# How far a gathering GpSimd may run ahead in the last two of three passes

## The chip, the cores and the metric

The kernel runs on one core of a Trainium2 chip. The time is that of the device for one execution, in microseconds (us), and stands as a median of several runs. Engines are named PE (TensorE, matmul; PEld is its weight load), DVE (VectorE), ACT (ScalarE), POOL (GpSimd) and SP (SyncE, which only issues DMAs here).

## The reference

A graph has 6250 nodes with 128 features and 100000 edges sorted by destination. Two layers of graph convolution are followed by one attention layer; both blocks end in a residual and a layer norm.

```
norm = dinv[src] * ew * dinv[dst]                    # dinv = 1/sqrt(deg), self-loops added
h  = relu(segment_sum((x@W1)[src] * norm, dst) + b1)
h  = sigmoid(segment_sum((h@W2)[src] * norm, dst) + b2)
x2 = layernorm(x + h)
z  = x2 @ fc_w.T;  rh = edge_attr @ fc_r_w.T
e  = leaky(z[src]@a0 + z[dst]@a1 + rh@a2)            # one score for each edge
alpha = softmax of e over the edges of each dst
agg = segment_sum(alpha * (z[src] + rh), dst)
out = layernorm(x2 + relu(agg + z @ loop_w))
```

## The kernel before

The edges are cut into 782 tiles of 128, and the tiles into 98 groups of 8. Each of the three sums over edges is one pass over the groups. In a pass, GpSimd fetches the source rows of each tile with one indirect DMA (128 rows, a gather), from x1_d in pass 0, h1_d in pass 1 and x2_d in pass 2, into `ring`. The ring has 18 groups (R) in passes 0 and 1 and 12 (R2) in pass 2. VectorE builds a one-hot matrix S of the destinations, weighted (`build_S`, L1608), and PE multiplies gathered rows by it into a window of PSUM (`sum_group`, L858; in pass 2 also the edge attributes, L860). After the last matmul of a group PE raises the semaphore `summed`.

Not all tiles are gathered. Sets of 32 tiles are permuted by source and looked up in a copy of the table in SBUF: ACT makes one-hots (`slot_onehot`, from a broadcast load of low_d that SP issues), PE looks rows up (`look_up`, L898), ACT copies them, VectorE makes slots (`make_slots`, L1681) and PE sums them (`sum_slots`, L910). Pass 0 has six such sets and gathers 74 groups, pass 1 nine sets and 62 groups (590 and 494 gathers). In pass 2 three sets (12 groups: 38 to 41, 62 to 65, 86 to 89) are treated in a like way, and 86 groups are gathered (686 gathers).

Each engine has its program written out; semaphores are the only tie. GpSimd's program is `gathers` for pass 0, 1 and 2 (L704 to L728). Ahead of a group it waits until its place in the ring has been summed, ahead of each gather until the one six before it has landed. A pass's gathers begin when the last blocks of its table are stored.

During pass 1 and after it come the picks: each edge needs the score z[dst]@a1 of its destination. `begin_pick` (L1825) compares a broadcast load of destination bits (dlo_d, issued by SP, 512 KB for a pair of groups after pass 1) with the partition index, PE multiplies with a small table (`pick`, L944), and `end_pick` (L1834) sums the result and raises `picked`, once for two groups, 49 times in all. 36 pairs are done within pass 1; the other 13 follow it, with three dot products of edge attributes (`rh_dot`, L1709) and the tables of nodes (`node_table`, L1797 to L1812) between them. Then pass 2's softmax starts: chunks of 2, then 4 groups. `scores(c)` (L1917) reads the gathered rows of its chunk and of one tile of the next (17 tiles for chunk 0, up to the 49th for chunk 1), and `softmax` (L1955 to L1978) gives the weights for `build_S`.

Of the kernel before, what the change touches and what calls it, by code (L numbers as in the profile page):

```python
# [16 lines left out]
G = -(-T // GT)  # L17
# [11 lines left out]
R = 18  # L29
# [22 lines left out]
def tiles(q):  # L52
    return range(q * GT, min((q + 1) * GT, T))
# [147 lines left out]
assert sorted(ORDER) == list(range(len(CH))) and all(XS[r] + 29 <= CLOSES[SETK[XR[r]]] for r in range(len(XR)))  # L201
assert all(XS[r] + 28 <= XS[r + 1] and X_AT[r] + 1 < CHUNK[XC[r]] for r in range(len(XR) - 1))
LANES = 6
PARTS = {G - 2: (0, 4, GT), G - 1: (0, 3, 5, T - (G - 1) * GT)}


# [31 lines left out]
def build(nc, x, src, dst, edge_attr, edge_weight, W1, b1, W2, b2, fc_w, fc_r_w, attn_w, loop_w, out):  # L238
    ctx = ExitStack()
    with ctx:  # L240
# [3 lines left out]
        def sem(name):  # L244
            return ctx.enter_context(nc.semaphore(name))
# [173 lines left out]
        def s(name):  # L419
            if name not in sems:  # L420
                sems[name] = sem(name)
            return sems[name]

        landed = [sem(f"landed{j}") for j in range(LANES)]
        rh_loaded = [sem(f"rh_loaded{j}") for j in range(NR)]
# [8 lines left out]
        def turn(p, t):  # L434

            return sum(len(tiles(i)) for g in GL[:p] for i in g) + (GL[p] if p < 2 else GATHERED).index(t // GT) * GT + t % GT

        def ring_at(p, h):

            return (AT[p] + h) % R if p < 2 else GATHERED.index(h) % R2  # L440

        def await_rows(eng, p, ts):

            for i in [turn(p, t) for t in ts][-LANES:]:
                eng.wait_ge(landed[i % LANES], 16 * (i // LANES + 1))

# [9 lines left out]
        def stored(sems, k):  # L456

            return sems[k % 2], 16 * (k // 2 + 1)

        def any_wide(eng):  # L460
            eng.wait_ge(s("flag_made"), 1)
            return eng.If(eng.value_load(flag[0:1, 0:1], min_val=0, max_val=1) != 0)

        def ecols(g):
            return bass.ds(g * GT, GT)
# [228 lines left out]
        @block.gpsimd  # L694
        def _(pool):
            nc.gpsimd.memset(srcR[:, EB - 1, :], 0).then_inc(s("pads_set"), 1)
            nc.gpsimd.memset(dstR[:, EB - 1, :], int(FAR)).then_inc(s("pads_set"), 1)
            nc.gpsimd.memset(ewR[:, EB - 1, :], 0.0).then_inc(s("pads_set"), 1)
            nc.gpsimd.iota(iota_i, [[1, NARROW]], base=0, channel_multiplier=0).then_inc(s("iota_made"), 1)
            nc.gpsimd.iota(pidx_i[:, :], [[1, 1]], base=0, channel_multiplier=1).then_inc(s("iota_made"), 1)  # L700
            nc.gpsimd.memset(rows[:, NB - 1, 0:D], 0.0).then_inc(s("pads_set"), 1)
            nc.gpsimd.iota(baseI, [[GT, TC]], base=-MARGIN, channel_multiplier=0).then_inc(s("iota_made"), 1)

            def gathers(p, table, width):  # L704
                for h, q in enumerate(GL[p] if p < 2 else GATHERED):
                    gg = AT[p] + h
                    if p == 0 and h == R0:
                        pool.wait_ge(s("x1_stored"), 16 * 7)
                    if p == 0 and h == R - 9:
                        pool.wait_ge(s("setup_done"), 1)  # L710
                        pool.wait_ge(s("dpad_stored"), 64)
                    if p == 2 and h >= R2:
                        pool.wait_ge(s("summed"), AT[2] + GATHERED[h - R2] + 1)
                    elif p < 2 and gg >= R:
                        pool.wait_ge(s("summed"), gg - R + 1)
                    for k, t in enumerate(tiles(q)):
                        i = turn(p, t)
                        if i >= LANES:
                            pool.wait_ge(landed[i % LANES], 16 * (i // LANES))
                        pool.indirect_dma_start(ring[:, ring_at(p, h if p < 2 else q), k, 0:width], None, (x if p == 0 and h < R0 else table)[:, :],  # L720
                                                bass.IndirectOffsetOnAxis(ap=srcC[:, t:t + 1], axis=0)).then_inc(landed[i % LANES], 16)
                    if p == 0 and h == P // GT - 1:
                        pool.wait_ge(s("cols_copied"), 7)

            pool.wait_ge(s("cols_copied"), 1)
            gathers(0, x1_d, D)
            pool.wait_ge(*stored(h1_stored, NA - 2))
            pool.wait_ge(*stored(h1_stored, NA - 1))  # L728
            gathers(1, h1_d, D)
            pool.wait_ge(*stored(x2_stored, NA - 2))  # L730
            pool.wait_ge(*stored(x2_stored, NA - 1))
            gathers(2, x2_d, XW)

            def wide_gathers(n, phase, table, width, stored):
                pool.wait_ge(stored, 16)
                with pool.Fori(0, G) as g:
                    pool.wait_ge(s("wide_group"), g + (phase * G + 1))
                    pool.sem_inc(s("pool_passed"))
                    nc.gpsimd.tensor_copy(stageW, srcC[:, ecols(g)]).then_inc(s("wide_staged"), 1)
                    pool.wait_ge(s("wide_staged"), g + (n * G + 1))  # L740
                    pool.sem_inc(s("pool_passed"))
                    for k in range(GT):
                        pool.indirect_dma_start(wring[:, k, 0:width], None, table[:, :],
                                                bass.IndirectOffsetOnAxis(ap=stageW[:, k:k + 1], axis=0)).then_inc(s("wide_gathered"), 16)

            with any_wide(pool):
                pool.wait_ge(s("out_stored"), 16 * NA)
                nc.gpsimd.iota(baseWi, [[GT, TC]], base=-MARGIN, channel_multiplier=0).then_inc(s("wide_iota"), 1)
                wide_gathers(0, 1, x1_d, D, s("wide_x1_stored"))
                wide_gathers(1, 2, h1_d, D, s("wide_h1_stored"))  # L750
                wide_gathers(2, 3, x2_d, XW, s("wide_x2_stored"))
                wide_gathers(3, 4, x2_d, D, s("wide_x2_stored"))

        @block.tensor
        def _(pe):
# [86 lines left out]
            def sum_group(p, h):  # L842
                gg = AT[p] + h
                q = SEQ[gg][1]
                parts = PARTS[q] if p < 2 and q in PARTS else (0, len(tiles(q)))
                if p == 2:
# [1413 lines left out]
```

## Time and profile before

| | |
|---|---|
| Runs | 2405.14 us median of 3 (2404.65 to 2409.71) |
| The profiled execution | span 3348.6 us; no other time of it is given |
| Mean granted PE clock | 0.787 |
| Busy share | PE 61%, PEld 53%, DVE 55%, POOL 51%, ACT 28% |
| Instructions | 40819; 1781 of them on POOL |

The profiled execution is a single one, recorded by the hardware. Its span is 943.5 us longer than the median of the runs. In timelines a row is: start, length, engine, line, operation, out<-in, and in brackets the engine's idle time just before and what ended it. "issue" there is time in which the engine waited for nothing that the profile shows; "remote" or "unknown queue" is a wait whose releaser isn't known. Pass 0 ends, and pass 1's gathers begin, at 1179.7 us; pass 2's gathers begin at 2117.07.

### The profile page before, as it was taken

How to read it: one execution, taken by the hardware profiler on the slowest of the kernel's cores; microseconds unless marked ns; L12 is line 12 of the kernel's file. 1: busy time of each engine (PE TensorE's matmuls, PEld its weight loads, DVE VectorE, ACT ScalarE, POOL GpSimd, SP SyncE). 2: the span in 40 equal slices, each digit the busy share in tenths (PEclk: the TensorE clock that was granted, in tenths of full speed). 3: DMA queues.
4: the chain of work that ended last, by engine and by line, in shares of the span. 5: the costliest groups of instructions: out<-in, count | busy, mean ns of one | idle time of the engine just before them, and what ended most of it. 6: DMA issues, size and time to landing. Idle time of an engine off the chain costs nothing.

```text
span 3348.6 us, 40819 instructions
## 1 busy us (share of the span) xinstructions
PE 2044.2 (61%) x13384; PEld 1762.3 (53%) x13384; DVE 1834.8 (55%) x7005; ACT 946.7 (28%) x1754; POOL 1718.9 (51%) x1781
## 2 busy tenths in 40 slices
PE   1416444588888911177777888106677667756786
PEld 1315433566767811166666677005666666645675
DVE  3626435577779810156656687217654564546457
ACT  1316000122233300033333444101254225412541
POOL 7351666665550067466556500555766646663640
PEclk9857667798999955588988899557778778877888
DMA  4112221222221122123333332525343534443431
GB/s 118 30 42 66 69 61 47 61 61 63 60 62 32 51 76 53 41 74 86 99 103 102 93 91 80 138 62 147 97 103 97 134 93 102 108 117 79 103 97 34
DMA packets 272093, 270.54 MB, mean 81 GB/s; under 512 B 43454, under 2 KB 218709, under 8 KB 271862
## 3 DMA queue, kind: packets, MB, share of 16 engines
q1 hardware_dynamic: 201790, 143.87, 15.1%
q0 software_dynamic: 56640, 117.52, 14.8%
q10 hardware_dynamic: 13448, 6.47, 0.7%
q8 instruction: 112, 1.84, 0.2%
q14 instruction: 103, 0.84, 0.1%
HBM read 254.14 MB, written 13.97 MB: 80 GB/s over the span
## 4 chain that ended last, share of the span: by engine, by line
PE 35%; DVE 21%; another core or an unknown queue 21%; issue 15%; ACT 4%; SPq 1%; DMA 1%; POOL 1%; ACTq 0%; DVEq 0%; POOLq 0%
PE ps L858 9%; PE ps L910 8%; DVE SR L1608 5%; PE ps L860 3%; PE ps L898 3%; PE ps L1045 2%; DVE U L1709 2%; DVE SR L1681 2%; DVE SR L1571 1%; PE ps L885 1%; DVE U L1648 1%; PE ps L1029 1%; POOL ring L720 1%; PE ps L792 1%
## 5 line engine op out<-in xcount | busy, mean ns | idle before, releaser
L720 POOL DMA_INDIRECT ring<-x_d,srcC x1132 | 1109.7, 980 | 971.2 <-issue 579.0
L858 PE MATMUL ps<-SR,ring 128*128 128x128 f32 x3540 | 672.5, 320 | 205.0 <-issue 132.0
L858 PEld LDWEIGHTS ps<-SR,ring 128*128 128x128 f32 x3540 | 580.5, 231 | 238.9 <-issue 178.9
L720 POOL DMA_INDIRECT ring<-h_d,srcC x494 | 469.9, 951 | 457.1 <-DMA h_d<-Lb 170.9
L1681 DVE TENSOR_SCALAR SR<-iota_r,cols 128x288 f32<-128x288 f32 x735 | 365.0, 564 | 303.9 <-remote 226.6
L910 PE MATMUL ps<-SR 128*128 128x288 f32 x1470 | 416.6, 435 | 118.1 <-ACT SR L1232 75.3
L910 PEld LDWEIGHTS ps<-SR 128*128 128x128 f32 x1470 | 292.3, 205 | 212.7 <-ACT SR L1232 77.5
L860 PE MATMUL ps<-SR 128*128 128x128 f32 x1564 | 340.3, 312 | 40.8 <-issue 34.6
L1232 ACT COPY SR<-ps 128x512 f32<-128x512 f32 (+1 forms) x195 | 106.0, 561 | 758.4 <-remote 502.9
L860 PEld LDWEIGHTS ps<-SR 128*128 128x128 f32 x1564 | 279.6, 228 | 48.3 <-issue 48.0
L898 PE MATMUL ps<-rows,SR 128*128 128x128 f32 x1470 | 196.2, 285 | 122.5 <-ACT SR L1241 90.6
L898 PEld LDWEIGHTS ps<-rows,SR 128*128 128x128 f32 x1470 | 186.7, 200 | 134.0 <-ACT SR L1241 96.0
L1608 DVE TENSOR_SCALAR SR<-iota,rankC,ewC 128x128 f32<-128x128 f32 x940 | 253.3, 357 | 2.6 <-DVE U L1812 1.1
L1608 DVE TENSOR_SCALAR SR<-iota,rankC,cols 128x128 f32<-128x128 f32 x782 | 213.0, 355 | 14.7 <-issue 11.7
L720 POOL DMA_INDIRECT ring<-in_x_dram,srcC x144 | 137.3, 953 | 93.7 <-issue 90.5
L1571 DVE TENSOR_SCALAR SR<-iota_h,rankC 128x128 bf16<-128x128 bf16 x584 | 107.6, 260 | 125.9 <-issue 106.1
L1709 DVE SCALAR_TENSOR_TENSOR U<-SR,v2B 128x128 f32<-128x128 f32 x686 | 156.0, 286 | 34.3 <-DVE U L1709 18.1
L1239 ACT ACTIVATE SR<-SR,negp 128x512 bf16<-128x512 bf16 (+1 forms) x195 | 134.9, 692 | 112.0 <-remote 100.3
L811 PE MATMUL ps<-SR,cols 128*3 128x128 bf16 (+2 forms) x974 | 74.0, 237 | 110.7 <-issue 57.0
L1241 ACT ACTIVATE SR<-SR,negp 128x512 f32<-128x512 bf16 (+1 forms) x195 | 135.9, 697 | 6.4
L1963 DVE TENSOR_TENSOR_SCAN U<-U,ps 32x384 f32<-32x384 f32 (+2 forms) x27 | 25.4, 942 | 203.8 <-remote 115.7
L811 PEld LDWEIGHTS ps<-SR,cols 128*3 128x3 bf16 x974 | 60.0, 96 | 123.5 <-issue 65.0
(288 smaller groups left out, 2703.4 us busy)
## 6 DMA issues: line engine op xcount, KB each, us to landing
SR<-in_edge_attr_dram SPq DMA_DIRECT2D x97, 512.0 KB
SR<-low_d SPq DMA_DIRECT2D x90, 256.0 KB
U<-dlo_d SPq DMA_DIRECT2D x74, 256.0 KB
ring<-x_d,srcC POOLq DMA_INDIRECT x1132
ring<-h_d,srcC POOLq DMA_INDIRECT x494
SR<-dlo_d SPq DMA_DIRECT2D x12, 512.0 KB
ring<-in_edge_attr_dram SPq DMA_DIRECT2D x12, 512.0 KB
U<-lo_d SPq DMA_DIRECT2D x18, 256.0 KB
```

Source lines behind the costliest of these rows:

```text
L720: pool.indirect_dma_start(ring[:, ring_at(p, h if p < 2 else q), k, 0:width], None, (x if p == 0 and h < R0 else table)[:, :], bass.Indire ...
L811: last = nc.tensor.matmul(ps[6 + k % 2][0:3, lo:hi], ewP[:, t, :], SH[:, q % ND, j, w0:w0 + hi - lo], start=False, stop=t == LAST[k])
L858: last = nc.tensor.matmul(ps[(p * NA + k) % 2][:, at], ring[:, ring_at(p, h), j, 0:D], S[:, gg % NS, j, :], start=False, stop=stop)
L860: last = nc.tensor.matmul(ps[2 + k % 2][:, at], rh[:, q % NR, j, :], S[:, gg % NS, j, :], start=False, stop=stop)
L898: last = nc.tensor.matmul(ps[3 + m % 2][:, i * P:(i + 1) * P], ohS[:, m % 2, i * P:(i + 1) * P], rows[:, a, 0:D], start=True, stop=True)
L910: nc.tensor.matmul(ps[5][:, SLACK:SPAN], rowX[:, m % 2, i * P:(i + 1) * P], slotS[:, n % NQ, :], start=False, stop=a == NB - 1).then_inc(s ...
L1239: nc.scalar.activation(low, low, ACT.Abs, bias=negp[:, 0:1]).then_inc(s("low_apart"), 1)
L1241: return nc.scalar.activation(out, low, ACT.Relu, bias=negp[:, 1:2], scale=-1.0)
L1571: last = v.tensor_scalar(SH[:, q % ND, j, :], iota_h[:, :], rankC[:, t:t + 1], None, ALU.is_equal)
L1608: last = v.tensor_scalar(S[:, gg % NS, j, :], iota[:, :], rankC[:, t:t + 1], w[:, t:t + 1], ALU.is_equal, ALU.mult)
L1681: v.tensor_scalar(slotS[:, n % NQ, :], iota_up, slotD[:, RUNS[i], a:a + 1], slotW[:, RUNS[i], a:a + 1], ALU.is_equal, ALU.mult).then_inc(s ...
L1709: v.scalar_tensor_tensor(junk[:, n % NJ, :], attr, 1.0, v2B[:, :], ALU.mult, ALU.mult, accum_out=s2C[:, t:t + 1]).then_inc(s("rh_dotted"), 1)
```

## The change

In pass 1 a group's gathers now wait until all but 8 groups ahead of it have been summed (before: all but 18). In pass 2 GpSimd gathers the first two groups and then waits until `picked` has reached 49, all pairs. Pass 0 and the ring's places stay as they are.

```diff
 LANES = 6
+AHEAD = 8
...
                     if p == 2 and h >= R2:
                         pool.wait_ge(s("summed"), AT[2] + GATHERED[h - R2] + 1)
-                    elif p < 2 and gg >= R:
+                    elif p == 2 and h == 2:
+                        pool.wait_ge(s("picked"), -(-G // 2))
+                    elif p == 1:
+                        pool.wait_ge(s("summed"), gg - AHEAD + 1)
+                    elif p == 0 and gg >= R:
                         pool.wait_ge(s("summed"), gg - R + 1)
```

Here p is the pass, h the number of the group within the pass, gg its number over all passes, and G is 98.

## Rows read from the trace of the kernel before

**Rows 1.** The page, part 4: the chain that ended last, shares of the span.
```profile
PE 35%; DVE 21%; another core or an unknown queue 21%; issue 15%; ACT 4%; SPq 1%; DMA 1%; POOL 1%; ACTq 0%; DVEq 0%; POOLq 0%
```

**Rows 2.** Windows: us, then busy (xcount) of PE, PEld, DVE, ACT, POOL, clock, DMA.
```profile
1000.00:1176.00 176.00, 157.24 (x1062) 137.00 (x1062) 149.95 (x467) 60.78 (x114) 5.91 (x6) 0.97 0.15 44
1205.00:1404.00 199.00, 19.65 (x58) 12.71 (x57) 1.72 (x3) 2.50 (x4) 139.38 (x148) 0.52 0.19 49
2130.00:2253.00 123.00, 2.59 (x56) 2.06 (x56) 6.85 (x35) 0.00 (x0) 82.19 (x87) 0.50 0.29 67
```

**Rows 3.** Timeline of the setup, VectorE: start, length, line, form, count, idle before.
```profile
84.24 0.25 DVE L1571 TENSOR_SCALAR SR<-iota_h,rankC 128x128 bf16<-128x128 bf16 x1 [1.15 <-issue]
...
107.34 22.52 DVE L1571 TENSOR_SCALAR SR<-iota_h,rankC 128x128 bf16<-128x128 bf16 x138 [0.45 <-issue]
```

**Rows 4.** Timeline of the start of pass 1: PE, ACT and VectorE.
```profile
1224.16 0.37 PE L898 MATMUL ps<-rows,SR 128*128 128x128 f32 x1 [2.43 <-issue]
...
1290.04 0.72 ACT L1239 ACTIVATE SR<-SR,negp 128x512 bf16<-128x512 bf16 x1 [100.25 <-remote]
...
1387.98 0.57 DVE L1681 TENSOR_SCALAR SR<-iota_r,cols 128x288 f32<-128x288 f32 x1 [194.92 <-remote]
```

**Rows 5.** Chain of waits by line in 1000:1176, 0:1180, 1180:2107 and 2107:3349.
```profile
by line: PE ps L910 20.4%; PE ps L858 15.5%; PE ps L885 8.2%; PE ps L898 7.6%; DVE SR L1681 7.2%; DVE SR L1608 6.8%; DVE U L1648 4.4%; PE ps L872 3.3%; PE ps L840 2.2%; PE ps L932 2.2%; issue 1.9%; DVE Lb L1722 1.9%; DVE U L1637 1.8%; PE ps
by line: issue 18.9%; another core or an unknown queue 15.9%; PE ps L910 7.9%; PE ps L858 6.9%; DVE SR L1608 6.2%; DVE SR L1571 3.6%; PE ps L885 3.5%; PE ps L898 2.8%; DVE U L1648 2.8%; POOL ring L720 2.2%; DVE SR L1681 2.1%; PE ps L872 1.9
by line: another core or an unknown queue 29.8%; PE ps L910 19.6%; PE ps L858 11.9%; issue 9.0%; PE ps L898 7.1%; DVE SR L1608 4.0%; DVE SR L1681 3.6%; ACT SR L1239 1.5%; PE ps L944 1.0%; SPq L574 1.0%; PE ps L840 1.0%; SPq L505 0.7%; ACT L
by line: another core or an unknown queue 19.7%; issue 17.1%; PE ps L858 8.3%; PE ps L860 8.1%; PE ps L1045 5.3%; DVE U L1709 4.9%; DVE SR L1608 4.3%; PE ps L1029 2.1%; PE ps L1033 2.0%; PE ps L1020 1.9%; DVE U L1970 1.5%; DVE U L1972 1.5%;
```

**Rows 6.** GpSimd's gathers: three of pass 2's start, then line L720 with all starts.
```profile
2117.07 1.10 POOL L720 DMA_INDIRECT ring<-x_d,srcC  x1 [181.26 <-issue]
...
2120.15 0.94 POOL L720 DMA_INDIRECT ring<-x_d,srcC  x1 [1.98 <-issue]
...
2237.73 0.95 POOL L720 DMA_INDIRECT ring<-x_d,srcC  x1 [0.30 <-issue]
...
L720 POOL DMA_INDIRECT ring<-x_d,srcC x1132: 938/944/2452, 316.5 to 3240.5; - x189
L720 POOL DMA_INDIRECT ring<-h_d,srcC x494: 938/944/1522, 1179.7 to 1934.9; - x165
```

**Rows 7.** Timeline of VectorE: the end of the picks, first and second scores.
```profile
2254.40 1.00 DVE L1825 TENSOR_SCALAR U<-SR,pidx 128x1024 bf16<-128x1024 bf16 x2
...
2255.43 0.99 DVE L1825 TENSOR_SCALAR U<-SR,pidx 128x1024 bf16<-128x1024 bf16 x2
...
2258.28 0.49 DVE L1825 TENSOR_SCALAR U<-SR,pidx 128x1024 bf16<-128x1024 bf16 x1 [0.22 <-DVE U L1812]
...
2260.04 0.20 DVE L1834 TENSOR_REDUCE s1C<-ps 128x14 f32<-128x42 f32 x1 [0.35 <-PE ps L944]
...
2261.13 0.18 DVE L1917 TENSOR_TENSOR cols<-ring,s1C 128x17 f32<-128x17 f32 x1
...
2280.79 0.21 DVE L1917 TENSOR_TENSOR cols<-ring,s1C 128x32 f32<-128x32 f32 x1
```

**Rows 8.** Timeline: last gather of pass 1's first group, and PE, released by it.
```profile
1188.50 0.94 POOL L720 DMA_INDIRECT ring<-h_d,srcC  x1 [0.30 <-issue]
...
1191.21 0.58 PE L792 MATMUL ps<-iota_r,zero_h 1*128 1x512 bf16 x1 [15.69 <-DMA ring<-h_d,srcC]
```

**Rows 9.** Lines of VectorE in 2110:2262: busy us, mean ns, idle before.
```profile
L1825 DVE TENSOR_SCALAR U<-SR,pidx 128x1024 bf16<-128x1024 bf16 x24 | 11.8, 498 | 118.6 <-remote 95.5 <-issue 21.1 <-DMA SR<-dlo_d 1.2
...
L1709 DVE SCALAR_TENSOR_TENSOR U<-SR,v2B 128x128 f32<-128x128 f32 x24 | 5.3, 283 | 0.0
```

**Rows 10.** DMA queues in 2115:2130: packets, MB, share of 16 engines.
```profile
q1 hardware_dynamic: 864, 2.69, 53.6%
q0 software_dynamic: 252, 0.54, 14.8%
```

## The prediction

> **What bounds the kernel now.** I read the totals first. The profiled execution spans 3348.6 us, and no engine is busy for more than 61% of it (the page's first part, in the table above). The runs shown take 2405.14 us (median), so 943.5 us of the profiled execution are not in a timed run; what lies around the span could only widen that. So the first question is which idle time of the trace exists in a timed run at all.
>
> The chain of waits gives 63% of the span to work of engines and DMAs (35+21+4+1+1+1), 2110 us, and 36% to an unknown releaser and to "issue" [rows 1]. If the work is the same in a timed run, 2405 − 2110 = 295 us are left for all waiting, against some 1205 us in the trace. Two stretches alone, 1205 to 1404 and 2130 to 2253, are 322 us long and hold 20 and 3 us of PE work and 2 and 7 us of DVE work [rows 2]. They can't both be real at full size beside normal waiting elsewhere.
>
> What kind of stall is it? In the setup, while GpSimd gathers without pause, VectorE starts the same 0.25 us comparison every 1.40 us, with "issue" ahead of it; at 107.34 us 138 of them run in 22.52 us, 0.16 each [rows 3]. Most of these wait for no semaphore. At the start of pass 1 a matmul of PE starts 2.43 us after the one before it, with "issue" ahead; then ACT sits 100.25 us and VectorE 194.92 us [rows 4]. From 1000 to 1176 GpSimd issues 6 gathers in all, PE and DVE are 89% and 85% busy, and the chain has 1.9% of issue [rows 2, 5]. So instructions of every engine are slowed to a fixed pace while gathers run back to back, and this lags a burst by some 15 us (gathers end at 2237.73, two pick pairs at 2254.40 and 2255.43 run freely) [rows 6, 7]. I read it as a cost of recording the trace, because 295 us have no room for it. The mechanism isn't visible; the arithmetic is the reason.
>
> What is left to bound a timed run? GpSimd starts a gather every 1.25 us (0.94 plus 0.30) whatever else happens: 96 of them from 2117.07 to 2237.73 [rows 6]. Pass 1 has 494 gathers, 617 us; pass 2 has 686, 856 us. The chain without its two kinds of waiting gives pass 1 (1180 to 2107) 61.2% of 927 = 567 us and pass 2 (2107 to 3349) 63.2% of 1242 = 785 us [rows 5]. So in both later passes the gathers are slower than everything else. Check: pass 0 without its waits is 65.2% of 1180 = 769; then 617, some 7 for the last sums, 20 from the last sums of pass 1 (2097) to the first gather of pass 2 (2117.07), 856, and 15 for the end: 2284 us, 121 below the runs. Close enough to take GpSimd as the bound of passes 1 and 2, not to prove it. My sum is therefore made as a difference against 2405, not against 3349.
>
> **Pass 1: at most 8 groups ahead.** The old wait was there too (summed ≥ gg−17); only its number changes, so no instruction is added. It delays a gather only when GpSimd is more than 8 groups (80 us) ahead. In the trace it is: 148 gathers run between 1205 and 1404 while PE has 20 us of work [rows 2]. In a timed run gathers are the slower side (10.0 us a group against 567/62 = 9.1), so the lead never grows and the wait passes. The last 4 groups carry no slot work and are summed faster; 8 groups of lead cover them. If PE or DVE is the bound instead, a full ring of 8 still feeds them. Nothing earlier can start either: pass 2's gathers wait for x2. Cost 0; bounds −5 (less traffic beside the broadcast loads) and +5.
>
> **Pass 2: two groups until all picks are done.** Behind the new wait stand gathers 17 to 686. It is one wait more on GpSimd, which issues nothing else. Who waits for them: VectorE's first scores cover 17 edge tiles, and the 17th lies in group 2. Before, all 96 gathers of the ring were issued between 2117.07 and 2237.7 beside the picks [rows 6]. After: the second gather starts at 2120.15, the 16th at 2120.15 + 14 × 1.25 = 2137.6, and GpSimd is free at 2138.6. When would the picks end without the recording stall? VectorE's work in them is 26 comparisons at 0.49 (12.8), 13 reductions at 0.20 (2.6), the rh dots of three groups (5.3) and three tables: the last one lies between 2256.4 and 2258.28, 1.9 us [rows 7, 9]. Together 26 us. Consecutive pairs at free pace are 1.03 us apart, which gives 24 us as a lower end (13 × 1.03 + 5.3 + 5.7). The 9 further pair loads of 512 KB (4.7 MB) ran at 2.69 MB in 15 us beside the gathers [rows 10], so 26 us, mostly beside that work; I allow up to 33 us. So picks end at 2115.8 + 26 to 33 = 2142 to 2149, and GpSimd stands still for 3 to 10 us. The first scores then wait for one gather: 0.94 to make it and some 1.8 to land (a group's last gather ended at 1189.44, PE was released by it at 1191.21 [rows 8]), instead of following 1 us after the last pick (2260.04 to 2261.13) [rows 7]. With GpSimd as the bound of pass 2 that standstill shifts every later gather and the end: +3 to +10, I take +6. The four far groups of each set (no gathers) let GpSimd catch up by 40 us, but what it catches up with has been late since the first chunk, so the delay isn't won back. Upper end: as long as the picks last in the trace (144.4 us), the pause would be 122 us; lower end −2.
>
> The trace shows transfers sharing engines: from 2115 to 2130 gathers take 14.8% and the loads 53.6% of the 16 DMA engines [rows 10]. The Trainium skill (DMA: Bandwidth & Descriptors, "Queues, rings and completion order") has each DMA engine serve its rings in turn, packet by packet, so loads alone go faster. By that rule the picks would end up to 2 us sooner; I don't count it.
>
> Sum: 0 + 6 = 2411 us for the likeliest case, its own range 2407 to 2419.
>
> **Rivals.**
> (1) The stalls are real in timed runs. Then the full-speed run at the start of pass 1 stops after 8 + 2 groups, at 1180 + 100 = 1280 instead of 1389, saving about 110; the picks, stalled for 123 us by 87 gathers, end about 106 sooner, of which the refill of ten groups at full speed (80 gathers at up to 1.2) takes back up to 95. That is −121 to −216: 2189 to 2284. For: the trace as it stands. Against: 295 us of room. A tenth to a sixth of it could live in that room, since PE's chain work is inflated by a mean clock of 0.79: −12 to −36, 2369 to 2393. Chances 7% and 15%. The Trainium skill (Runtime: NRT & Kernel Launch, "The ~15µs preamble/postamble breakdown") puts the profile's total about 6 us over the time of a run, whatever the kernel. By that rule a timed run would be near 3342 us and every stall real; the measured 2405 decides against it here.
> (2) GpSimd has slack in timed runs (gathers quicker than 1.25 when nothing is recorded). Then the first two chunks bite: in the trace the second scores come 19.7 us after the first [rows 7], but need 33 gathers after the picks, up to 41 us. Old start: 49 gathers from 2117, 63 us, against 32 + 20. That leaves the second chunk 10 to 22 us later: 2415 to 2427. 13%, of it 3% within 0.2%.
> (3) The pause hides: picks end with the 16th gather, or the bound lies in work that has 10 us to spare at the first chunk. 2403 to 2409. 15%. That the change doesn't act at all belongs here: with gathers as the bound the first part really does nothing.
>
> **How the numbers follow.** A difference under 0.2% (4.8 us) can't be told from none. Likeliest case 50% (35 slower, 15 within), (1) 22% faster, (2) 10 slower and 3 within, (3) 15 within. So faster 0.22, same 0.33, slower 0.45. Range 2375 to 2432: it leaves out the full size of (1), a part of its small version, and a tail of long picks.
>
> **What would show it.** In the changed profile: the full-speed run of pass 1 ends near 1280, VectorE's 195 us wait falls to about 90; the picks take about 40 us instead of 144, and after them gathers run at full speed and slow the first sums. The profiled span should fall to between 3130 and 3230 while the timed median hardly moves: that opposition is the test of my first step. It is wrong if both fall by the same 100 us or more. The pass 2 step is wrong if GpSimd finds picks already done after its 16th gather, or if taking out this wait alone doesn't bring the timed run back.

## The result, and the profile after

The changed kernel takes 2410.11 us (median of 20 runs, 2405.26 to 2417.56); beside it the kernel before takes 2405.80 us (20 runs, 2403.52 to 2409.88). The ratio is 1.0016 (95% interval 1.0009 to 1.0024): slower by 2 to 6 us, and 2411 had been predicted.

The profile of the changed kernel looks nothing like that of before. Its span is 2404.7 us, and the same execution took 2406.48 us as a run. Its page, first part (busy), second part (tenths in 40 slices) and the chain:

```profile
span 2404.7 us, 40820 instructions
...
PE 1837.1 (76%) x13384; PEld 1626.4 (68%) x13384; DVE 1817.9 (76%) x7005; ACT 947.0 (39%) x1754; POOL 1743.7 (73%) x1781
...
POOL 7777777777776377777777774777777777777771
...
PE 30%; DVE 29%; POOL 22%; issue 12%; DMA 3%; ACT 3%; SPq 2%; ACTq 0%; DVEq 0%; POOLq 0%
POOL ring L725 22%; PE ps L915 8%; PE ps L863 8%; DVE SR L1613 6%; DVE SR L1576 4%; PE ps L903 3%; DVE SR L1686 2%; PE ps L890 2%; DVE U L1714 1%; DVE U L1653 1%; PE ps L865 1%; PE ps L877 1%; DMA ring<-in_edge_attr_dram 1%; PE ps L845 1%; DMA ring<-x_d,srcC 1%
```

The unknown releaser, 21% of the chain of before [rows 1], is gone, and gathers, 1% there, are 22%. GpSimd is 70 to 80% busy in all but four slices: that is what "a gather, a gap of 0.30 us, the next gather" looks like in tenths. The slices that dip are the two changes of pass and the end. The stretch that held 6 gathers in the trace of before [rows 2] holds 139 (windows; the columns are those of rows 2):

```profile
1000.00:1176.00 176.00, 154.38 (x1079) 133.90 (x1078) 142.39 (x463) 81.22 (x129) 133.49 (x139) 0.93 0.42 121
```

All gathers by table, with shortest, median and longest in ns and first and last start, then GpSimd's waits (us in total, times, longest):

```profile
L725 POOL DMA_INDIRECT ring<-x_d,srcC x1132: 940/944/2456, 194.3 to 2354.5; - x189
L725 POOL DMA_INDIRECT ring<-h_d,srcC x494: 938/944/1590, 817.3 to 1441.3; - x165
L725 POOL DMA_INDIRECT ring<-in_x_dram,srcC x144: 940/947/1691, 5.8 to 193.0; - x144
...
POOL ring L725 <- issue: 589.8, 1723, 41.9
POOL ring L725 <- DMA ring<-x_d,srcC: 10.4, 32, 0.9
POOL ring L725 <- DVE s1C L1839: 3.3, 1, 3.3
POOL ring L725 <- DVE srcC L1499: 3.2, 1, 3.2
POOL ring L725 <- DMA ring<-h_d,srcC: 2.8, 8, 0.7
POOL ring L725 <- PE ps L863: 0.9, 3, 0.3
```

This answers [rows 6]. Where GpSimd's time goes, from these starts and two rows of its timeline (817.26 us after 41.95 us idle, 1463.73 us after 21.45): 5.8 us to the first gather, about 769 in pass 0, 43 to the next pass, 624.1 in pass 1, 22.4 to pass 2, 890.7 in it, 50.2 from the last gather to the end. These make 2405. No engine has a row of waits to compare with it: GpSimd waits for data 21 us in all. So one engine, at one instruction every 1.30 us (1.27 in pass 1), sets the length of all three passes, and only the two changes of pass (64 us) and the tail (50 us) belong to others. The chain alone would not have said so: it follows one releaser at each step, gives PE and VectorE 59% here, and its share of gathers lies anywhere from 18% to 43% in the profiles of the experiments below.

The changed place itself, GpSimd and VectorE at the end of the picks (answers to [rows 6, 7]):

```profile
1463.73 1.10 POOL L725 DMA_INDIRECT ring<-x_d,srcC  x1 [21.45 <-issue]
1466.81 0.94 POOL L725 DMA_INDIRECT ring<-x_d,srcC  x1 [1.98 <-issue]
...
1484.52 1.15 POOL L725 DMA_INDIRECT ring<-x_d,srcC  x1 [0.30 <-issue]
...
1488.54 0.20 DVE L1839 TENSOR_REDUCE s1C<-ps 128x14 f32<-128x42 f32 x1 [0.35 <-PE ps L949]
...
1489.01 0.96 POOL L725 DMA_INDIRECT ring<-x_d,srcC  x1 [3.34 <-DVE s1C L1839]
...
1493.63 0.18 DVE L1922 TENSOR_TENSOR cols<-ring,s1C 128x17 f32<-128x17 f32 x1 [4.13 <-DMA ring<-x_d,srcC]
```

GpSimd ends its 16th gather at 1485.67, 21.9 us after its first began, and stands still until the last pick: 3.34 us, of which 0.30 is the usual gap. The first scores follow 5.1 us after the last pick, waiting for the 17th tile.

### The profile page after: what moved, and what is told of

The parts are those of the page before. It is cut to its first block, busy times and chain, and to the rows that moved or that the text cites. A ratio compares the mean times of both kernels' runs of the same rounds, so it can differ in the third digit from the quotient of the medians.

```text
span 2404.7 us, 40820 instructions
## 1 busy us (share of the span) xinstructions
PE 1837.1 (76%) x13384; PEld 1626.4 (68%) x13384; DVE 1817.9 (76%) x7005; ACT 947.0 (39%) x1754; POOL 1743.7 (73%) x1781
## 4 chain that ended last, share of the span: by engine, by line
PE 30%; DVE 29%; POOL 22%; issue 12%; DMA 3%; ACT 3%; SPq 2%; ACTq 0%; DVEq 0%; POOLq 0%
POOL ring L725 22%; PE ps L915 8%; PE ps L863 8%; DVE SR L1613 6%; DVE SR L1576 4%; PE ps L903 3%; DVE SR L1686 2%; PE ps L890 2%; DVE U L1714 1%; DVE U L1653 1%; PE ps L865 1%; PE ps L877 1%; DMA ring<-in_edge_attr_dram 1%; PE ps L845 1%; DMA ring<-x_d,srcC 1%
## 5 line engine op out<-in xcount | busy, mean ns | idle before, releaser
L725 POOL DMA_INDIRECT ring<-x_d,srcC x1132 | 1123.0, 992 | 371.5 <-issue 356.8
L863 PE MATMUL ps<-SR,ring 128*128 128x128 f32 x3540 | 617.2, 307 | 102.4 <-DVE SR L1613 56.8
L863 PEld LDWEIGHTS ps<-SR,ring 128*128 128x128 f32 x3540 | 540.2, 220 | 126.4 <-issue 62.1
L915 PE MATMUL ps<-SR 128*128 128x288 f32 x1470 | 380.3, 411 | 0.0
L915 PEld LDWEIGHTS ps<-SR 128*128 128x128 f32 x1470 | 275.9, 193 | 71.8 <-issue 2.4
L865 PE MATMUL ps<-SR 128*128 128x128 f32 x1564 | 319.5, 299 | 6.0 <-DVE SR L1613 6.0
L865 PEld LDWEIGHTS ps<-SR 128*128 128x128 f32 x1564 | 262.6, 216 | 6.2 <-issue 6.0
L725 POOL DMA_INDIRECT ring<-in_x_dram,srcC x144 | 144.6, 1004 | 46.8 <-issue 43.3
L1000 PE MATMUL ps<-ident,cols 128*32 128x128 f32 (+2 forms) x81 | 17.9, 345 | 124.5 <-DVE cols L1925 108.2
L1357 ACT ACTIVATE U<-U 32x384 f32<-32x384 f32 (+2 forms) x27 | 14.1, 523 | 226.8 <-DVE U L1970 226.7
L1576 DVE TENSOR_SCALAR SR<-iota_h,rankC 128x128 bf16<-128x128 bf16 x584 | 97.9, 291 | 0.2
```

The lines of the kernel that those rows point to most:

```text
L863: last = nc.tensor.matmul(ps[(p * NA + k) % 2][:, at], ring[:, ring_at(p, h), j, 0:D], S[:, gg % NS, j, :], start=False, stop=stop)
L865: last = nc.tensor.matmul(ps[2 + k % 2][:, at], rh[:, q % NR, j, :], S[:, gg % NS, j, :], start=False, stop=stop)
L915: nc.tensor.matmul(ps[5][:, SLACK:SPAN], rowX[:, m % 2, i * P:(i + 1) * P], slotS[:, n % NQ, :], start=False, stop=a == NB - 1).then_inc(s ...
L1576: last = v.tensor_scalar(SH[:, q % ND, j, :], iota_h[:, :], rankC[:, t:t + 1], None, ALU.is_equal)
```

## The experiments

Twelve kernels ran. "Before" is the median of the kernel before on the same chip in the same set. Each edit is against the kernel before.

**The kernel before, profiled again** (no edit).

> The kernel before, unchanged, profiled once more. Theory A (the long profile of the kernel before was a disturbed recording, not something its bursts of gathers do): the span is about 2400 us, gathers start every 1.25 to 1.3 us from the first to the last, and VectorE's wait at the start of pass 1 is a few us, not 195. Theory B (full-speed gathers beyond 8 groups ahead slow the recording): the span is again near 3350 us, with the long wait of VectorE at the start of pass 1. Its time against itself: ratio 1.000 within 0.001 by both.

2407.61 us, ratio 0.9998 (0.9987 to 1.001). The new profile spans 2408.4 us. Its page, the gathers of passes 0 and 2 with those of pass 1, and the comparisons of the setup:

```profile
span 2408.4 us, 40819 instructions
...
POOL 7777777777776377777777774777777777777771
...
L720 POOL DMA_INDIRECT ring<-x_d,srcC x1132: 940/944/2448, 194.3 to 2358.2; - x189
L720 POOL DMA_INDIRECT ring<-h_d,srcC x494: 940/944/1585, 817.4 to 1441.7; - x165
...
71.60 64.28 DVE L1571 TENSOR_SCALAR SR<-iota_h,rankC 128x128 bf16<-128x128 bf16 x384
```

Same program, same time in a run, 940 us less in the profile. The profiled execution took 2410.16 us as a run, 1.8 more than its span. 384 comparisons run at 0.167 us each beside gathers without a pause; in the first profile they came every 1.40 us [rows 3]. VectorE's longest wait at the start of pass 1 is 23.1 us (for PE, until 853.91): not the "few us" that I expected, but far from 195. So the long stalls belong to that one profiled execution. Since its time as a run isn't given, it isn't shown whether the recording or the execution itself was slow.

**Pass 1's limit alone.**

```diff
-                    elif p < 2 and gg >= R:
+                    elif p == 1:
+                        pool.wait_ge(s("summed"), gg - AHEAD + 1)
+                    elif p == 0 and gg >= R:
```

> Only the first part of the change: at most 8 groups ahead in pass 1, the wait for the picks taken out. Theory: gathers bound pass 1, the lead stays under 8 groups, so the wait always passes: 0 us, ratio 0.999 to 1.001, and GpSimd shows no wait on PE of more than 1 us in all in pass 1. Rival (the limit of 8 starves PE where sums run in bursts): +2 to +5 us, and GpSimd waits for summed in pass 1.

2408.01 us against 2407.99, ratio 1.0002 (0.9992 to 1.0012). Pass 1's gathers take 624.4 us from first to last start, as with the old limit (624.3), and none of them waits for PE. The limit costs nothing that can be measured.

**Pass 2's wait alone, measured twice** (pass 1 as before):

```diff
+                    elif p == 2 and h == 2:
+                        pool.wait_ge(s("picked"), -(-G // 2))
```

> Only the second part: pass 1 with the old 18 groups, the wait for the picks in. Theory: the whole loss is here, GpSimd stands still 3 to 4 us (3.34 in the profile after) and the time is +3 to +5 us over the kernel before, ratio 1.0012 to 1.0021. Rival (the loss is in pass 1): ratio within 0.0005 of 1.

> Pass 2's wait after two groups alone, once more, since its first measurement could not tell +2 us from none. Theory (each us of GpSimd's standstill is about a us at the end; 0, 13 and about 26 us of it gave 0, +14 and +26 us): with 3 to 4 us of standstill +3 to +4 us, ratio 1.0012 to 1.0017. Rival (a standstill of a few us is absorbed, and the changed kernel's +4.3 us was partly something else): ratio under 1.0008.

2407.95 us against 2407.99, ratio 1.0008 (0.9998 to 1.0017), and 2408.59 against 2407.20, ratio 1.0005 (0.9995 to 1.0014): by the ratios +1.9 and +1.2 us, by the medians 0 and +1.4. GpSimd stands still for 4.33 us in both profiles:

```profile
1489.67 0.96 POOL L725 DMA_INDIRECT ring<-x_d,srcC  x1 [4.33 <-DVE s1C L1839]
...
1490.71 0.96 POOL L725 DMA_INDIRECT ring<-x_d,srcC  x1 [4.33 <-DVE s1C L1839]
```

Both expectations missed: the first ratio lies under the 1.0012 that I expected, the second also under the 1.0008 that I gave to the rival. Neither interval leaves out 2 us, neither leaves out 0; the first ends at +4.1 us and the second at +3.4, so a us of time for each of the 4 us that GpSimd stood still longer lies at the edge of the first and outside the second.

**No group, one group, four groups before the wait** (h == 0, h == 1, h == 4 in the line above).

> The wait for the picks stands before group 0 of pass 2 instead of group 2, so no gather of pass 2 runs beside the picks; pass 1 as before. Theory (gathers bound pass 2, so each us GpSimd stands still is a us of the end): the picks end about 25 us after x2 is stored, so the time is +22 to +26 us, ratio 1.009 to 1.011, a little less if the picks end sooner without gathers beside them. Rival (the start of pass 2 has slack): under +12 us.

> Pass 2 fetches one group before it waits for the picks; pass 1 as before. Theory (each us of standstill is a us at the end): GpSimd is done about 12 us after its first gather, the picks about 25 after it, so it stands still some 13 us: +11 to +14 us, ratio 1.0045 to 1.006, on a line between two groups (3 to 4 us of standstill) and none (about 25 us, +26 measured). Rival (the first chunk needs 17 tiles, so a fixed number of gathers late counts and not the standstill): +4 or less, or +20 or more.

> Pass 2 fetches four groups, not two, before it waits for the picks; pass 1 as before. Theory (the pause costs only the time GpSimd stands still: 32 gathers of 1.30 us are 41 us, the picks end about 26 us after the first): no standstill, 0 us, within 2 us of the kernel before. Rival (the wait itself or the order costs): +3 or more, as with two groups.

2434.36, 2420.81 and 2407.32 us; ratios 1.0115 (1.0098 to 1.0132), 1.0067 (1.0052 to 1.0082) and 1.0001 (0.9992 to 1.0011). GpSimd's gather behind the wait and the first scores, in the kernel with no group ahead:

```profile
1492.23 0.94 POOL L725 DMA_INDIRECT ring<-x_d,srcC  x1 [48.99 <-DVE s1C L1839]
...
1516.64 0.18 DVE L1922 TENSOR_TENSOR cols<-ring,s1C 128x17 f32<-128x17 f32 x1 [24.49 <-DMA ring<-x_d,srcC]
```

with one group ahead:

```profile
1491.35 0.96 POOL L725 DMA_INDIRECT ring<-x_d,srcC  x1 [13.13 <-DVE s1C L1839]
...
1507.87 0.18 DVE L1922 TENSOR_TENSOR cols<-ring,s1C 128x17 f32<-128x17 f32 x1 [16.03 <-DMA ring<-x_d,srcC]
```

and with four, where no such wait shows and the scores follow the last pick (1492.18) by 1.1 us:

```profile
1493.27 0.18 DVE L1922 TENSOR_TENSOR cols<-ring,s1C 128x17 f32<-128x17 f32 x1
```

Side by side (us; 48.99 holds the usual gap between the passes, 21.4 to 22.8 in all profiles but one, so 27 of it are new; the third column is last start of pass 2 minus last start of pass 1):

| groups ahead | standstill | last gather after pass 1's last | ratio − 1 in us |
|---|---|---|---|
| 4 | 0 | 911.0 | +0.2 |
| 2, this change | 3.3 | 913.1 | +3.9 |
| 2, alone, twice | 4.3 | 914.1; 915.5 | +1.9; +1.2 |
| 1 | 13.1 | 922.7 | +16 |
| 0 | 27 | 937.9 | +28 |

Without a wait in pass 2 the third column is 909.7 to 916.5 us (seven profiles; the kernel before, whose pass 2 began about 4 us late in its profile, has 916.5). So it shows the two long pauses but can't show those of 3 to 4 us.

The starts within pass 2 can. From its first gather to its last it is 887.2 to 889.5 us where nothing stops GpSimd after the first (eight profiles; a ninth, of pass 1's limit of 2, has 892.1, with gathers that last longer on the whole), and 890.7, 891.7, 893.0 and 900.4 us with 3.3, 4.3, 4.3 and 13.1 us of standstill. From the 17th gather to the last it is 865.2 to 867.3 us in twelve profiles (869.9 in that ninth), whatever the standstill before. So what GpSimd misses at the start of pass 2 it never makes up, small pauses included. The time of the whole follows clearly for the two long pauses: 26.4 us by the medians for none ahead, where 22 to 26 were expected (28 by the ratio), and 13.8 for one ahead (16 by the ratio, above the expected 14). For pauses of 3 to 4 us it disappears in what else differs from execution to execution, such as the gap before pass 2 and the tail.

**Pass 1's limit at 2 and at 4** (AHEAD = 2, AHEAD = 4 in the edit of the second experiment).

> The limit of pass 1 set to 2 groups, nothing else changed. Theory (in pass 1 the gathers are the slower side, so the lead over the sums is about one group and a limit rarely bites): 0 to +6 us, 2408 to 2414, pass 1's gathers from first to last 625 to 632 us. Rival (the lead is used now and then, and what is lost isn't won back): over +12 us, 2420 or more.

> The limit of pass 1 set to 4 groups, nothing else changed. Theory (what counts is the lead that the gathers really reach, which a limit of 2 cut into nine times for 12.7 us in all): between a limit of 8 (0 us) and of 2 (+8.6 us), near the first: 0 to +3 us, with under 3 us of GpSimd waiting for PE in pass 1. Rival (any limit below the ring's own costs in proportion): +5 us or more.

2415.52 us, ratio 1.0037 (1.0023 to 1.0051), for 2; 2406.37, 0.9997 (0.9986 to 1.0008), for 4. The limit of 2 cost 8.6 us by the medians, over my 0 to 6 and under the rival's 12; the profile is of its longest run, 2422.15 us. GpSimd's waits in pass 1 with a limit of 2, and two of them:

```profile
POOL ring L723 <- PE ps L861: 12.7, 9, 3.1
...
1054.39 0.95 POOL L723 DMA_INDIRECT ring<-h_d,srcC  x1 [2.49 <-PE ps L861]
...
1066.31 0.95 POOL L723 DMA_INDIRECT ring<-h_d,srcC  x1 [2.22 <-PE ps L861]
```

and in the whole kernel with a limit of 4:

```profile
POOL ring L723 <- PE ps L861: 1.8, 6, 0.3
```

With 2, nine gathers waited for PE, 12.7 us together, and pass 1's gathers took 635.6 us instead of 624.1 to 626.6. With 4, none waited longer than the usual gap of 0.30. So GpSimd bounds pass 1 too, and the lead that it uses is between 2 and 4 groups. A limit of 8 has room for twice that.

**The tail: last chunks of one group, of four, of three and three.**

```diff
-CH = [2] + [4] * 22 + [2] * 4
+CH = [2] + [4] * 22 + [2] * 3 + [1] * 2
```

```diff
-CH = [2] + [4] * 22 + [2] * 4
+CH = [2] + [4] * 22 + [2] * 2 + [4]
...
-E_AT[-3] = A_AT[-3] = CHUNK[-4] - 2
+E_AT[-2] = A_AT[-2] = CHUNK[-3] - 2
```

The third has `[2] + [3] * 2` at the end and the same second edit.

> The kernel before with its last softmax chunk of two groups cut into two of one group each, nothing else. Theory (the gathers set the end of pass 2, and the 50 us after the last gather hold the softmax, one-hots and sums of a whole chunk): a smaller last chunk shortens that tail by 3 to 6 us, 2402 to 2405. Rival (one more softmax takes back what the shorter chunk saves, or the tail is the end of the kernel's last sums in PE): 0 or up to 5 us slower.

> The kernel before with its last two softmax chunks of two groups merged into one of four; the early placing of one chunk's scores in PE's order moves by one chunk so that it stays at the same group. Theory (what the 50 us after the last gather hold is VectorE's and PE's chain, with two softmax rounds of 8 us in it, not the gathers): with one round after the last gather, softmax ends at +12 us instead of +26 us, the sums of four groups take 14 us, the end comes 6 to 12 us sooner: 2395 to 2401. Rival (the bigger chunk's sums start only then and take back what the round saved, as splitting the chunk cost 0 to +5): within 3 us of before, or slower.

> The kernel before with its last three chunks of two, two and two groups cut into three and three. Theory (the rounds after the last gather count): one softmax round of the last chunk after it, the previous chunk's landed some 29 us before; 5 to 10 us sooner, 2397 to 2402, near the merged chunk of four. Rival: within 3 us of before, or slower.

| last chunks | time, before beside it | ratio (interval) | last gather to end of span |
|---|---|---|---|
| 2, 2 (before) | | | 50.2 |
| 2, 1, 1 | 2410.18, 2406.97 | 1.0011 (0.9999 to 1.0024) | 52.2 |
| 2, 4 | 2406.13, 2406.68 | 0.9997 (0.9985 to 1.0009) | 47.2 |
| 3, 3 | 2404.48, 2406.68 | 0.9987 (0.9978 to 0.9996) | 48.9 |

All three missed what I expected of them in size, the first perhaps in sign too, and all three came out by their medians as the rivals said. With the last chunks left as they were, the tail is 47.6 to 52.4 us in ten profiles; so of the three tails no one is shown to be longer or shorter. VectorE in the tail of the kernel before (last gather at 2358.2), its second profile: scores, end of softmax, one-hots, twice over, then the last layer norm:

```profile
2361.88 0.25 DVE L1917 TENSOR_TENSOR cols<-ring,s1C 128x15 f32<-128x15 f32 x2
...
2369.63 0.17 DVE L1978 COPY cols<-ps 128x16 f32<-128x16 f32 x1 [0.38 <-PE ps L1001]
...
2376.91 0.17 DVE L1917 TENSOR_TENSOR cols<-ring,s1C 128x13 f32<-128x13 f32 x1
...
2384.75 0.17 DVE L1978 COPY cols<-ps 128x14 f32<-128x14 f32 x1 [0.32 <-PE ps L1001]
2384.96 3.68 DVE L1608 TENSOR_SCALAR SR<-iota,rankC,cols 128x128 f32<-128x128 f32 x14
...
2399.65 0.56 DVE L1991 SCALAR_TENSOR_TENSOR Lb<-ps,rows 128x384 f32<-128x384 f32 x1 [11.01 <-PE ps L1088]
```

and with a last chunk of four groups (last gather at 2355.7):

```profile
2359.27 0.25 DVE L1917 TENSOR_TENSOR cols<-ring,s1C 128x15 f32<-128x15 f32 x2
...
2371.62 0.19 DVE L1978 COPY cols<-ps 128x30 f32<-128x30 f32 x1 [0.34 <-PE ps L1001]
...
2394.09 0.56 DVE L1991 SCALAR_TENSOR_TENSOR Lb<-ps,rows 128x384 f32<-128x384 f32 x1 [11.51 <-PE ps L1088]
```

Two softmax rounds of 7.8 us stood behind the last gather. With one round, which takes 12.4 us for four groups, the softmax is over 15.9 us after the last gather instead of 26.6. But the sums of four groups follow it then, not of two, and the layer norm starts 38.4 us after the last gather instead of 41.5: of 10.7 us won, 3.1 reach the end in this pair of profiles, and 0.6 us (within −3.6 to +2.2) the time. That a round more (2, 1, 1) costs about 2 us isn't shown: its interval holds 0. Three and three is the only version here whose interval lies below the kernel before, 0.04% to 0.22%, 2 to 3 us by median and ratio; as one of three tried, and so near to none, it would need a second measurement.

## Why the prediction was right, point by point

- **"943.5 us of the profiled execution are not in a timed run": right, its reason not borne out.** That 295 us had no room for the stalls was arithmetic and held. What I made of it, instructions slowed by the recording "while gathers run back to back", fell: in thirteen further profiles of the same or nearly the same programs, gathers run back to back all along and nothing slows, and the kernel before itself spans 2408.4 us. The first profiled execution was disturbed as a whole. Its trace holds 15,325 semaphore events; the second of the same program holds 43,842. Why is open. For the same reason the test that I named, a profiled span of 3130 to 3230 us, failed: it is 2404.7, and neither a fall of pass 1's full-speed run nor of VectorE's wait can be read in it.
- **"GpSimd is the bound of passes 1 and 2, at 1.25 us a gather": right as the bound, the pace too small.** It bounds pass 0 as well, which I had left to others at 769 us; that 590 gathers take just that is chance, since my figure was a sum mostly of the other engines' work. The pace is 1.30 in pass 2 (890.7 us for 685 steps), not 1.25: 856 was too low by 35. The 121 us that my check lacked are these 35, 7 in pass 1, 49 ahead of pass 1 (6 to the first gather and 43 between the passes, where I had none) and 35 in the tail (50 instead of 15), less 5 between passes 1 and 2. The pauses with one group and with none ahead show the bound: what delays the gathers delays the end.
- **Pass 1, cost 0, bounds −5 and +5: right.** Alone it measures +0.02 us by the medians (ratio 1.0002, 0.9992 to 1.0012). My reason, a lead that "never grows", was too simple: the lead reaches two to four groups, and a limit of 2 costs 8.6 us.
- **Pass 2, 16 gathers in 21.5 us, picks of 26 to 33, standstill 3 to 10, +6: right, at the low end.** 21.9 us, picks over 24.8 us after the first gather (25 to 32 predicted), standstill 3.3 us. So the term was 2 to 3 us too large against this standstill. The change measures +4.3 us, the wait alone +1.2 and +1.9. That 2411 lies only 0.9 us from 2410.11 is luck: the kernel before took 2405.8 beside it and not 2405, and the change measured more than its standstill. By the prediction's own line (under 0.2%, 4.8 us, counts as none) the result falls under "same", which had 0.33, and not under "slower", which had 0.45, though its interval leaves out 0. The first scores wait longer than I worked out: 4.6 us from the start of gather 17, not 2.7, since its landing took 3.7 us and not 1.8. That changes nothing, since gather 18 and the rest don't wait for it.
- **Up to 2 us for picks that have the DMA engines to themselves: not seen.** From pass 2's first gather to the last pick it is 24.2 us with one group beside them, 24.8 and 25.9 with two, 24.8 with four, 24.9 to 26.3 with no limit. With no gather at all beside the picks the last one comes 48.9 us after pass 1's last gather; with some it is 46.6 to 51.9. The Trainium skill (DMA: Bandwidth & Descriptors, "Queues, rings and completion order") has each DMA engine serve its rings in turn. The gain that I had worked out from that isn't seen here, and the spread of one pick burst, 2.1 us, is as large as it.
- **Rivals.** Real stalls (22%): none in the thirteen further profiles, whose spans lie 1.8 us or so under the times of the same executions. Slack in GpSimd (13%): none in pass 2; a loss at the first chunk only would not have moved the last gather. "The pause hides" (15%): no for the pauses of one and no group; for 3 to 4 us it isn't hidden from the gathers, which take that much longer from the first to the last of pass 2, but in the time the two runs of that edit alone can't tell it from 0 or from +3.

What stays open: the whole change measures 2 to 6 us, its parts alone 0 and 1 to 2. The intervals overlap (parts summed: up to some 5), so nothing needs a further cause, and nothing excludes one of a us or two.

## What to carry to other kernels

Where a profiled span and the timed runs differ by hundreds of us, take the profile again before explaining any row of it; an argument from the total survived here, and every mechanism read from the stalls did not. When one engine issues without a pause from start to end, price a change by how long that engine stands still: here a limit that it never reached was free, and a pause of 13 or 27 us cost its length. Behind such an engine's last instruction the tail is a different problem: 10.7 us won at one step of it did not move the time measurably.

## What the runs showed of the hardware

A gather is 0.94 us at its median, and the next starts 0.30 us after it, with or without a wait to pass. That makes 1.25; the measured pace is 1.30 since some gathers last longer: busy time of all 1770 is 1742 us, 0.98 each, so 71 us in all. The two longest lie beside one VectorE operation (changed kernel, timeline):

```profile
1584.51 1.90 DVE L1941 TENSOR_TENSOR ring<-iota,ring 128x1666 bf16<-128x1666 f32 x1
1584.77 2.45 POOL L725 DMA_INDIRECT ring<-x_d,srcC  x1 [0.30 <-issue]
...
1872.39 1.90 DVE L1941 TENSOR_TENSOR ring<-iota,ring 128x1666 bf16<-128x1666 f32 x1
1872.64 2.46 POOL L725 DMA_INDIRECT ring<-x_d,srcC  x1 [0.30 <-issue]
```

Both gathers began 0.25 us into it and ended 0.8 us after it, 1.5 us late. By the Trainium skill (SBUF — State Buffer, "SBUF: two separate sides") a GpSimd-issued DMA can't write its descriptors while VectorE holds the port that the two share; these rows agree. The operation runs three times in the kernel; the third time a gather that began 1.3 us into it also ended 0.8 us after it, but the one before, begun with the operation, took its usual 0.94. The three late gathers hold 3.6 of the 71 us. The rest is spread over some 200 gathers of over 1.0 us, beside many other VectorE operations, and why they last longer isn't shown. No run took any of those operations away, so it isn't measured what another choice of instruction on VectorE would bring; the 71 us are an estimate of the upper limit.
